# Two GNN layers on one core: row buffers of the scatter stage moved, its base rows loaded sooner, masks and first products placed elsewhere, a wider key match in the last three iterations

## The reference

```python
h = jnp.maximum(_layernorm(x), 0.0)
x = x + gat(h)      # layer 0
    # h @ W_embed, per edge logit = leaky_relu(dot_src[src] + dot_dst[dst]),
    # prob = softmax over the edges of one dst, out = segment_sum(h[src] * prob, dst) + h @ W_lin + bias
h = jnp.maximum(_layernorm(x), 0.0)
x = x + mpnn(h)     # layer 1
    # row, col = src, dst
    # m = relu(concat(h[row], h[col], bond) @ W1 + b1) @ W2 + b2
    # m = m * sigmoid(bond @ Wa + ba);  h + segment_sum(m, row)
```

## Time and profile before

| | us |
|---|---|
| runs | 1535.42, 1535.7, 1541.37 |
| median | 1535.7 |
| the profiled execution | 1536.59 |
| its span, first to last instruction | 1534.6 |
| busy in it: PE, DVE, ACT, POOL | 1021.9, 1100.7, 782.2, 1139.4 |
| mean granted TensorE clock, share of full | 0.87 |

### The profile page before, as it was taken

The page is one execution under the profiler, slowest core; times in us unless marked ns, Lnnn a source line. Parts: engine busy times, 40 slices in busy tenths (PEclk is TensorE's granted clock), DMA queues, the critical chain, the costliest instruction groups (busy, mean ns, idle before and its releaser), DMA issues.

```text
span 1534.6 us, 23152 instructions
## 1 busy us (share of the span) xinstructions
PE 1021.9 (67%) x5651; PEld 760.7 (50%) x5651; DVE 1100.7 (72%) x3786; ACT 782.2 (51%) x2168; POOL 1139.4 (74%) x992
## 2 busy tenths in 40 slices
PE   0777777777777764655554477667777677677663
PEld 0555565655655544555554344444545444454442
DVE  2889898989889888988888655555555556555551
ACT  0788888888888885666655322222222222222220
POOL 5777777777777713777777668888888888888884
PEclk9999999999999985767776689898898899889996
DMA  8477777777777744555554333333333333333332
GB/s 268 129 215 215 223 212 221 213 219 227 214 227 214 222 161 152 180 179 171 173 174 152 97 47 50 49 50 52 50 50 51 52 50 52 50 50 50 50 40 21
DMA packets 177809, 202.28 MB, mean 132 GB/s; under 512 B 22219, under 2 KB 130767, under 8 KB 177599
## 3 DMA queue, kind: packets, MB, share of 16 engines
q1 hardware_dynamic: 119421, 122.80, 24.8%
q0 software_dynamic: 56496, 71.62, 24.7%
q10 hardware_dynamic: 1810, 6.93, 1.4%
HBM read 90.62 MB, written 109.84 MB: 131 GB/s over the span
## 4 chain that ended last, share of the span: by engine, by line
POOL 40%; issue 27%; DMA 20%; DVE 8%; PE 2%; ACT 1%; POOLq 0%; SPq 0%; DVEq 0%; ACTq 0%
POOL out_dram L1169 17%; POOL XE L1155 8%; DMA out_dram<-BD,sx 7%; POOL out_dram L1115 4%; POOL O L443 3%; POOL XN L443 3%; POOL R L443 3%; POOL XE L443 3%; DMA O<-in_x_dram,ix 2%; DMA XE<-in_x_dram,ix 2%; DMA R<-in_x_dram,ix 2%; DMA XE<-out_dram,ixs 2%; DMA out_dram<-BS,sx 2%; DMA XN<-in_x_dram,ix 2%; DVE H L889 1%
## 5 line engine op out<-in xcount | busy, mean ns | idle before, releaser
L1115 POOL DMA_INDIRECT out_dram<-BD,sx x196 | 205.2, 1047 | 115.2 <-issue 60.8
L1155 POOL DMA_INDIRECT XE<-out_dram,ixs x196 | 209.0, 1066 | 62.0 <-issue 57.4
L1269 DVE TENSOR_SCALAR XN<-bank,bwc 128x128 f32<-128x128 f32 x196 | 55.2, 344 | 270.8 <-PE bank L1396 270.8
L715 ACT ACTIVATE BD<-BD,nmr,rstd 128x128 f32<-128x128 f32 x392 | 170.8, 488 | 67.7 <-DVE nmr L576 67.7
L1169 POOL DMA_INDIRECT out_dram<-BS,sx x100 | 160.1, 1601 | 42.6 <-issue 35.9
L1054 PE MATMUL bank<-BD 128*128 128x128 f32 x392 | 110.6, 377 | 120.5 <-DVE BD L932 120.5
L1169 POOL DMA_INDIRECT out_dram<-TS,sx x96 | 153.7, 1601 | 37.3 <-issue 27.6
L1377 PE MATMUL bank<-ident,XE 128*128 128x128 f32 x196 | 40.8, 344 | 190.4 <-DMA XE<-out_dram,ixs 190.4
L777 PE MATMUL bank<-ident,BD 128*128 128x128 f32 x588 | 108.2, 295 | 80.0 <-DVE BD L569 77.9
L1054 PEld LDWEIGHTS bank<-BD 128*128 128x128 f32 x392 | 87.0, 274 | 131.4 <-issue 131.4
L789 PE MATMUL bank<-wes,TS 128*128 128x132 f32 x392 | 101.1, 341 | 71.0 <-ACT TS L726 68.5
(11 more groups left out here) (229 smaller groups left out, 3246.8 us busy)
## 6 DMA issues: line engine op xcount, KB each, us to landing
out_dram<-BD SPq DMA_DIRECT2D x98, 512.0 KB, 3.0
base_rows<-BD SPq DMA_DIRECT2D x49, 256.0 KB, 3.8
BD<-base_rows SPq DMA_DIRECT2D x49, 256.0 KB, 3.5
H<-BD SPq DMA_DIRECT2D x49, 256.0 KB, 3.2
XE<-in_x_dram SPq DMA_DIRECT2D x13, 512.0 KB, 6.6
BD<-bond_rows SPq DMA_DIRECT2D x49, 128.0 KB, 2.1
bond_rows<-in_edge_attr_dram ACTq DMA_DIRECT2D x1, 6250.0 KB, 23.6
XN<-in_x_dram SPq DMA_DIRECT2D x12, 512.0 KB, 6.1
```

Source lines behind the costliest of these rows:

```text
L715: last = nc.scalar.activation(OT[u][:, g, w:w + D], OT[u][:, g, w + D:w + 2 * D], ACT.Relu, bias=nmr[:, slot, t:t + 1], scale=rstd[:, slot ...
L1115: pool.indirect_dma_start(out, bass.IndirectOffsetOnAxis(sx[:, u, c:c + 1], 0), RO4[u][:, c, :], None, bounds_check=lim, oob_is_err=False) ...
L1155: pool.indirect_dma_start(XS4[u][:, c, :], None, halves, bass.IndirectOffsetOnAxis(ixs[:, u, c:c + 1], 0), bounds_check=lim, oob_is_err=Fa ...
L1269: last = nc.vector.tensor_scalar(MS[:, c * D:(c + 1) * D], bM[:, c * D:(c + 1) * D], bwc[:, u % 2, c:c + 1], None, ALU.mult)
```

## The change

1. `RO4[0..3]` lies at columns 3072, 0, 1024, 2048 of `BD`: buffer 0 in slot 1's part, the others in slot 0's.
2. `rows_stored` takes the slots to wait for. DVE waits for slot 3 at the stage's start, for slot 1 before it writes row buffer 0, and for slots 0 and 2 before row buffer 1. ACT waits for slots 2 and 3, POOL for all.
3. SP issues the four first base loads ahead of the stores of iterations 47 and 48. The last iteration stores only partitions 22 to 127, which don't overlap iteration 47's, so its store has no wait for them.
4. The masks are computed in the last iteration of the rows, in two groups, ahead of `take` 0 and `take` 2.
5. The first iterations of messages: destination and bond products of iteration 0 go ahead of the source transposes, the keys of iteration 1 stand behind the first messages, and the transposes and hidden products of iteration 1 behind the first sums. ACT's copies follow.
6. In iterations 46 to 48 (`WIDE`) the key match runs over all four columns, so that no node stands in two columns of an iteration; the sums have sixteen products for eight; POOL has no wait between the two pairs. The spare rows are a set for each of the four columns.

```diff
-                nc.gpsimd.iota(spare[:, :], [[0, 2], [2 * P, 2]], base=2 * N + 1, channel_multiplier=2,
+                nc.gpsimd.iota(spare[:, :], [[2 * P, G4]], base=2 * N + 1, channel_multiplier=2,
...
-        def rows_stored(eng):
-            for u in range(4):
+        def rows_stored(eng, *slots):
+            for u in slots:
...
-                sp.dma_start(rows[:, 2 * half:2 * half + 2, :], OT[u][:, 2 * half:2 * half + 2, 0:4 * D]).then_inc(st_o[u][half], 16)
+                p0 = (NODES_PER_IT * ITS - N) // ROWS if isinstance(it, int) and it == ITS - 1 else 0
+                sp.dma_start(rows[p0:P, 2 * half:2 * half + 2, :], OT[u][p0:P, 2 * half:2 * half + 2, 0:4 * D]).then_inc(st_o[u][half], 16)
...
             store(ITS - 3, (ITS - 3) % 4, 1)
-            store(ITS - 2, (ITS - 2) % 4, 0)
-            store(ITS - 2, (ITS - 2) % 4, 1)
-            for half in range(2):
-                sp.wait_ge(st_o[(ITS - 2) % 4][half], 16 * (ITS // 4))
-            store(ITS - 1, (ITS - 1) % 4, 0)
...
-            store(ITS - 1, (ITS - 1) % 4, 1)
+            for it in (ITS - 2, ITS - 1):
+                for half in range(2):
+                    store(it, it % 4, half)
...
+                if isinstance(it, int) and it == ITS - 1:
+                    dve.wait_ge(ix_ready, ITS - 4)
+                    nc.vector.tensor_scalar(gsrc, gsrc, 2.0, None, ALU.mult)
+                    link(nc.vector.tensor_scalar(hend, nsame, -1.0, 1.0, ALU.mult, ALU.add))
                 take(it, u, k, 0)
...
-        RO4 = [BD[:, u * 1024:(u + 1) * 1024].rearrange("p (c w) -> p c w", w=W) for u in range(4)]
+        RO4 = [BD[:, a:a + 1024].rearrange("p (c w) -> p c w", w=W) for a in (3072, 0, 1024, 2048)]
...
+                if isinstance(it, int) and it < 2:
+                    rows_stored(dve, *((1,), (0, 2))[it])
                 need(10)
...
-            rows_stored(dve)
+            rows_stored(dve, 3)
...
+                    wide = isinstance(it, int) and it >= WIDE
+                    if (past(k) or u or pair) and not (wide and pair):
                         pool.wait_ge(ms_add, 32 * (2 * it + pair))
...
+            def wide_keys(it, u):
+                for c in range(G4):
+                    kc = key1[:, bass.ds(blk(it) * G4 + c, 1)]
+                    w = (1 + c) * P
+                    nc.vector.tensor_scalar(S4[it % 2][:, c * G4 * P:(c + 1) * G4 * P], bK[u % 2][:, :], kc, None, ALU.is_equal)
+                    nc.vector.scalar_tensor_tensor(junk4[:, c * G4 * P:c * G4 * P + w], bK[u % 2][:, 0:w], kc, upto4[:, G4 * P - w:],
+                                                   ALU.is_equal, ALU.mult, accum_out=cnt[:, c:c + 1])
...
+                if it == 0:
+                    act.wait_ge(ms_sum, 1)
+                    nc.scalar.copy(UPD[0], bU[:, :]).then_inc(ms_upd, 1)
+                    take_bond(1)
+                    take_dst(1)
+                    take_src(1)
+                    act.wait_ge(ms_keys, 2)
+                    columns(2)
...
+                wide = isinstance(it, int) and it >= WIDE
                 for c in range(G4):
-                    for b in (c // 2 * 2, c // 2 * 2 + 1):
+                    for b in range(G4) if wide else (c // 2 * 2, c // 2 * 2 + 1):
...
+                if it == 0:
+                    flip_dst(1, 1)
+                    flip(1, 1, 0)
+                    hidden_known(1)
+                    hidden_src(1)
```

More of the change, by code:

```diff
@@ L46, in gnn_program @@
     assert FULL == P - 1 and 0 < TAIL < COLS and ITS % 2 == 1
-    assert ITS == -(-N // NODES_PER_IT)
+    assert ITS == -(-N // NODES_PER_IT) and (NODES_PER_IT * ITS - N) % ROWS == 0
     PAD = N + 3 * P - 1
@@ L628, in body @@
                     measure_rows(it, u, 1)
+                if isinstance(it, int) and it == ITS - 1:
+                    nc.vector.tensor_tensor(hend[:, 0:COLS - 1], hend[:, 0:COLS - 1], hmask[:, 0:COLS - 1], ALU.mult)
+                    nc.vector.tensor_tensor(hend[:, COLS - 1:COLS], hmask[:, COLS - 1:COLS], hashead[:, :], ALU.mult)
+                    nc.vector.tensor_scalar(pen, same, -1.0, BIG, ALU.add, ALU.mult)
+                    nc.vector.tensor_scalar(penn, nsame, -1.0, BIG, ALU.add, ALU.mult)
                 take(it, u, k, 2)
@@ L1134, in gnn_program @@
         HDST = Rw[:, 1280:1280 + G4 * D]
+        WIDE = ITS - FETCH
+        S4 = [H[:, 8192 + n * 2048:10240 + n * 2048] for n in range(2)]
+        junk4, upto4 = H[:, 12288:14336], H[:, 14336:14336 + G4 * P]
         ld_s = [sem(f"ms_gathered{u}") for u in range(4)]
@@ L1271, in body @@
                 last.then_inc(ms_scaled, 1)
+                if isinstance(it, int) and it == WIDE - 2:
+                    nc.vector.tensor_copy(upto4[:, 0:P], ltri[:, 0:P])
+                    nc.vector.tensor_copy(upto4[:, P:2 * P], ltri[:, 0:P])
+                    nc.vector.tensor_copy(upto4[:, 2 * P:4 * P], ltri[:, :])
                 if upto(it, ITS - 2):
@@ L1324, in body @@
                     edge_rows(act, it + FETCH + 1, (u + FETCH + 1) % 4)
[L1325 to L1328 removed]
+                if it > 0:
+                    act.wait_ge(ms_sum, it + 1)
+                    if past(k):
+                        act.wait_ge(ms_add, 16 * G4 * (it - 3))
+                    nc.scalar.copy(UPD[u], bU[:, :]).then_inc(ms_upd, 1)
                 if upto(it, ITS - 3):
@@ L1338, in messages_scalar @@
             weight(0, 0)
-            for n in range(2):
-                take_dst(n)
-                take_src(n)
-                take_bond(n)
-                if n == 0:
-                    take_hidden(0)
-                act.wait_ge(ms_keys, n + 1)
-                columns(n + 1)
+            take_dst(0)
+            take_bond(0)
+            act.wait_ge(ms_keys, 1)
+            columns(1)
+            take_src(0)
+            take_hidden(0)
             every4(act, body)
@@ L1378, in flip, with hidden_known @@
                 last.then_inc(ms_flip, 1)
-            def hidden(it):
+            def hidden_known(it):
                 if past(it):
@@ L1400, in body @@
             def body(it, u, k):
-                if upto(it, ITS - 2):
-                    hidden(it + 1)
+                if 0 < it <= ITS - 2:
+                    hidden_known(it + 1)
+                    hidden_src(it + 1)
                 pe.wait_ge(ms_scaled, it + 1)
@@ L1420, in messages_tensor @@
             flip_dst(0, 0)
+            hidden_known(0)
             flip(0, 0, 0)
-            hidden(0)
+            hidden_src(0)
             messages(0)
-            flip_dst(1, 1)
-            flip(1, 1, 0)
             keys(1, 1, 0)
```

45 lines of the change are left out of this document (21 added, 24 removed).

## The result

| | before | after |
|---|---|---|
| median of 13 runs, us | 1538.38 | 1532.25 |
| lowest, highest | 1533.26, 1544.06 | 1528.84, 1535.46 |
| the profiled execution, span | 1536.59, 1534.6 | 1530.4, 1528.7 |
| ratio of the times, 95% interval | | 0.9956, 0.9944 to 0.9969 |

The forecast was 1523.0, from 1518.5 to 1529.5, so the measured time lies above its range. The gain is 6.8 us (0.44% of 1538.4) where 12.8 were expected. (Of the distance in the time itself, 2.7 us come from the kernel before, whose median is 1538.4 here and was 1535.7 in the three runs that the forecast started from.) The traces of the two kernels show where it stopped.

A forecast was written before the change was run, and what follows sets the result against it. POOL's own issue was taken as the bound, with real waits only at two starts and the end. Gains 4.8 + 4.0 + 4.0 = 12.8 us off 1536.6 give 1523.8, the median 0.9 lower: 1523.0, range 1518.5 to 1529.5.

The forecast's parts named there:

- Part 1: Scatter stage's start: idle before L983 removed and masks moved into VectorE's waits for PE, 4.8 us, from 4.2 to 5.0.
- the partial store of 106 partitions: Scatter stage's start: storing 106 partitions counted as no time, the last store landing 3 us early for 589.5.
- the three signs of being wrong: 196 scatters over 270 us; L983 still waiting for a store; idle before iteration 47's scatters growing over 2 us.
- The idle time before L983: Scatter stage's start: VectorE idles for layer 0's stores; narrower waits and earlier base loads gain 3.8 us.
- The masks: Before the softmax products: six mask instructions fit into two VectorE waits for PE, worth 0.5 to 1.0, taken as 1.0 us.
- Part 2: Message stage's start: reordered PE work brings first sums and POOL's first message scatter 4.0 us sooner, from 1.5 to 5.4.
- the rival that the first sums are paid back: Message stage's start: PE slow through iteration 1, leaving 1.5 us of the gain there; time 1525.4, chance 0.16.
- Part 3: Last three iterations: POOL drops the wait between pairs, less the wider sums' cost, 4.0 us, from 2.6 to 5.3.
- the rival of the high clock: Kernel's end: PE keeps its high clock, 5.74 us from last transposes to sums, gain there 5.3; time 1521.6, chance 0.17.
- The dropped waits: Iterations 47 and 48: back-to-back pairs save 2.26 us each, together 4.5; 15.3 us from 47's first scatter to the last.
- the price: Iteration 46: sixteen products for eight make PE's sums 1.95 us longer, charged in full against the dropped waits' gain.
- the slower rival: Scatter stage: POOL's issues stretched by VectorE's new phase, up to 37 us more over 196 scatters, time 1560; chance 0.03.

The follow-up runs named there:

- Part 1 alone: Changed kernel with iteration 48's 128-partition store behind iteration 47's landing, old message-stage start, matches in pairs to the end: 1531.25 us, ratio 0.9963 to before.
- the split version: Changed kernel with iteration 48's 106-partition stores cut into 96 and 10: 1524.18 us, ratio 0.9913 to before; run again 1525.45 us, 0.9911.
- the full store behind the old wait: Changed kernel, but iteration 48 stores all 128 partitions after waiting for iteration 47's stores: 1523.7 us, ratio 0.9907 to before.
- 105 and 1: Changed kernel with iteration 48's 106-partition stores cut into 105 and 1 partitions, on the slower third chip: 1696.72 us, one run.

## Why the prediction was wrong

**Part 1, the failed step.** The prediction put the partial store of 106 partitions at no time, and held it for 3 us early because it was issued no later than before. It reckoned a store by its issue and its bytes. Its landing of 6.1 us was that of 128 partitions; 106 run on two DMA engines and land some 18 us behind the release of the last. The wait for it, 6.62 us at L933, is what the forecast missed: 30.81 us in the table, and not 24.35, 6.46 us. This alone takes 12.8 to 6.3. None of the three signs of being wrong that the prediction named came, since none asked about the second base add; of the signs of being right, POOL's first scatter near 591.9 did not come (599.01).

**Part 1, the rest.** The idle time before L983 was put at 3.8 us; with a fast store the stretch is 28.14 - 24.35 = 3.8 shorter. The masks, put at 1.0, are 1.2. Part 1 alone was to be 4.8 and is 5.7 us by its ratio (0.0037 of 1537.5), 5.0 by the two stretches.

**Part 2.** Put at 4.0 us: 3.7 and 3.8 in the two executions of the changed kernel, 2.4 in one of the split version, by the slow first sums. Over all eleven executions with the new start it is 18.2 to 19.6 us from gather to scatter, and the first sums take 1.95 to 3.12. The range of 1.5 to 5.4 held all. Iteration 1's wait was 0.85 us, below the 1 us named; the rival that the first sums are paid back did not come.

**Part 3.** Put at 4.0, and 5.6 in the traces, near the rival of the high clock (5.3). The dropped waits gave what was forecast: 15.4 us from iteration 47's first scatter to the last, where 15.3 was named. Two things on the way there were otherwise. The first is the price. The 1.95 us of the wider sums were charged in full, but they are no cost at the high clock, where without them iteration 46's second pair holds iteration 47: 12.60 us from 46's first scatter to 47's, and 12.28 in part 1 alone (there at the low clock, and held by a landing too), against 11.6 and 12.1 with the wide sums. The prediction said that iteration 46's own wait gives nothing, which is so only at the clock of the earlier trace rows.

The second is the reason for the high clock, and here luck had a part. The prediction reckoned 3.1 us of idle time before the last gather's transposes. The changed kernel has 1.74, because iteration 46's own products had run at the low clock (its sums 7.31 us behind its transposes, not 5.74) and so ended later. Where iteration 46 ran at the high clock, in the two executions of the split version, the idle time was 3.17 us as reckoned, and the last gather's transposes were fast once and slow once.

**The sum with the parts' measured sizes.** 3.8 + 1.2 + 3.7 + 5.6 = 14.3, less 6.5 for the store is 7.8 us. Measured are 6.8 (0.9956) and 8.8 (0.9943). With a fast store 14.3 stand against 13.4 (0.9913) and 14.3 (0.9907). So the forecast of 12.8 was near what the change is worth without this store, with part 3 sized 1.6 us too low, and POOL's 196 scatters, the place of the slower rival, took 262.4 us, not over 270.

**A version faster than both.** The split in 96 and 10, or the full store behind the old wait, is 0.87% to 0.93% faster than before.

## What to carry to other kernels

Where an edit changes the number of partitions of a plain DMA, look for the divisor before the bytes: two stores of 106 partitions took 18 us where one of 128 had landed in 6, and 105 and 1 were not waited for. A store that nobody waited for can become the last thing when the waits are made narrower, so cost its landing, not its issue. And at an end where landings and sums take turns in holding POOL, cost both before charging either: what one loses the other may have taken anyway.

## What the runs showed of the hardware that was not expected

- Stores of 53 partitions moved 26 GB/s and stores of 106 partitions 51, with under one tenth and one tenth of the 16 engines busy; stores of 128 partitions, together with spills and base loads, had mostly 300 to 414 in the same view. Four stores of 53 partitions issued one after the other shared one engine.
- TensorE's clock at the end, behind the idle time before the transposes of the last two gathers, in the fourteen profiled executions. After 0.55 to 2.40 us the transposes were fast (0.66 us, the 2.4 GHz level) and the clock stayed high up to the sums, some 5.7 us after the transposes (4.8 where the sums stand ahead of the product). After 4.91 to 5.71 us, six times, the transposes were slow (1.11 to 1.12 us, 1.2 GHz). Between them both came: after 3.32 and 3.72 us the clock stayed high; after 3.66, 3.69, 3.70, 3.91 and 3.95 the transposes were fast but the clock fell behind them (sums 7.3 us after the transposes, granted clock 0.50 in 1484 to 1486 of the changed kernel), and so it did after 3.42, twice, with transposes of 0.68 and 0.74. After 3.17 us it stayed high in one execution of the split version and was low in the other, which made 1.5 us of the tail. So in this range the idle time alone does not decide, and fast transposes do not show that the clock stays high.

```profile
1489.30 0.66 PE L1410 MATMUL bank<-ident,XE 128*128 128x128 f32 x4 [3.17 <-DMA XE<-out_dram,ixs]
```

```profile
1489.96 1.12 PE L1410 MATMUL bank<-ident,XE 128*128 128x128 f32 x4 [3.17 <-DMA XE<-out_dram,ixs]
```

The first line is of the split version's timeline, the second of its second execution's.

- The third chip took 1717.5 us for before. Its granted TensorE clock from 20 to 560 us was 0.78 to 0.81, where the other two have 0.95 to 0.97, and the scatter stage took 303 to 310 us, not 262 to 268; the message stage took the same. What slows it was not tried.
